# Two attentions and two feed-forward layers: q and k in two f32r parts on paired 64-row tiles, and attention loops unrolled

## The chip, the cores and the metric

The kernel runs on one core of a Trainium2 chip. The core has a matrix engine (PE), whose weight loads are shown as an engine of their own (PEld), a vector engine (DVE), a scalar engine (ACT), a general one (POOL) and a queue engine (SP) that issues transfers. The metric is the device time of one execution in microseconds, lower is better.

## The reference

All in float32, x is [2, 1024, 512]. Four layers, each on a layer norm of x and added to it:

```python
x = x + attn_a(ln(x))     # q = x Wq; latent = x Wc; k = latent Wk; v = latent Wv; rope on q, k;
                          # softmax(q k / 4) v, then Wo; 32 heads of 16, not causal
x = x + ffn(ln(x))        # x W + bias + a LoRA product
x = x + attn_b(ln(x))     # qkv = x w_attn + b; causal; scores / 16 + slope * (key - query)
x = x + ffn(ln(x))        # the same weights as before
```

## The kernel before

`project_a` makes q, k and v of attention a, `attention` runs attention a, `output_and_ffn` the output product, the feed-forward layer and the projection for b, then `attention` and `output_and_ffn` run again for b.

**Parts.** q and k are written to memory as three bf16 parts (high, middle, low) whose sum is the float32 value. A product q k is one matmul over 96 rows: six blocks of 16 rows, q's parts (0,0,0,1,1,2) against k's (0,1,2,0,1,0). In scores three more rows carry minus the maximum of the query (three bf16 parts against ones), in b three more the alibi ramp. ACT makes high and middle (`high`, `middle`), DVE the differences (`less_high`, `low`).

**Groups.** `attention` goes through 16 groups of four heads. The memory for a group's q, k and v is a slot, and there are three. A group has units: pairs of a half of the queries (512) and a block of 128 keys, 16 units in a and 12 in b, where masked blocks are left out. For each unit PE computes the scores of four heads (`scores`, L410, in two pairs of heads; each pair's exponential is one ACT instruction, L470, over two PSUM banks) and the value products (`values`, L427: plain f32, four heads on four 32-column tiles, two passes each).

**Maxima ahead.** The softmax needs each query's maximum before its scores. So 13 units (b) or 11 (a) ahead, PE computes q k with queries on the partitions (`maxima`, L369) in pieces of 128 queries by up to 512 keys, 64 pieces a group in a and 48 in b, and DVE reduces each to a column (L492). These pieces go through three PSUM banks (`MXB`): a piece waits for `piece_taken` of the one three before it. When half of a group is reduced, DVE takes the negated maxima, POOL splits them in parts (four instructions in a chain), PE turns them (L377, one item in the same three banks), DVE copies (L505) and one SP transfer writes them to the rows of the slot (L297).

**Order.** Each engine's order is written out by hand. In a unit PE does: scores of two heads, some pieces, scores of two heads, some pieces, values of the unit before, the other pieces. In a that is four pieces a unit. In b the diagonal blocks get a mask: a matmul of an identity and a 128x128 bf16 mask (L367, L408) ahead of the product in the same bank.

**Loops.** The first group is peeled, the next twelve are a hardware loop on each engine (on PE, DVE and SP four turns of three groups), the last three are straight code.

Of the kernel before, what the change touches and what calls it, by code (L numbers as in the profile page):

```python
# [37 lines left out]
Q_PARTS = (0, 0, 0, 1, 1, 2)  # L51
K_PARTS = (0, 1, 2, 0, 1, 0)
SROWS = DH * len(Q_PARTS)
SLOTS = 3
PEELED_FRONT = 1
LOOPED = 12


def wait_past(e, sem, value):

    if not isinstance(value, int) or value > 0:
        e.wait_ge(sem, value)


class Slot:
# [3 lines left out]
    QK_WORDS = GH * S // 2  # L69
    V_WORDS = 8 * GH * VW  # L70
    WORDS = 2 * QK_WORDS + V_WORDS

    def __init__(self, memory, rows, v_memory=None):

        self.rows = rows
        self.crow = rows - 3
        self.al = self.crow - SROWS
        n = self.QK_WORDS
        self.q = memory[0:rows, 0:n].bitcast(BF16)
        self.k = memory[0:rows, n:2 * n].bitcast(BF16)  # L80
        self.v = (memory[:, 2 * n:self.WORDS] if v_memory is None else v_memory).rearrange("p (k c) -> p k c", k=8)

    def load_q_row(self, e, r, q_d, g, loaded):

        e.dma_start(self.q[DH * r:DH * (r + 1), :].rearrange("d (n t) -> d n t", t=CHUNK),
                    q_d[Q_PARTS[r], bass.ds(g * 2 * GD, 2 * GD), :].rearrange("(n d) t -> d n t", d=DH),
                    ).then_inc(loaded, 16)

    def load_k_row(self, e, r, k_d, g, loaded):

        e.dma_start(self.k[DH * r:DH * (r + 1), :].rearrange("d (h t) -> d h t", h=GH),
                    k_d[K_PARTS[r], bass.ds(g * GD, GD), :].rearrange("(h d) t -> d h t", d=DH),
                    ).then_inc(loaded, 16)

    def load_q(self, e, q_d, g, loaded):
        for r in range(len(Q_PARTS)):
            self.load_q_row(e, r, q_d, g, loaded)

    def load_k(self, e, k_d, g, alibi_d, loaded):
        for r in range(len(K_PARTS)):  # L100
            self.load_k_row(e, r, k_d, g, loaded)
        if self.al:
            e.dma_start(self.k[SROWS:self.crow, :], alibi_d[bass.ds(g * self.al, self.al), :]).then_inc(loaded, 16)
# [5 lines left out]
    def set_rows(self, e, ones_d, done):  # L109

        e.dma_start(self.k[self.crow:self.rows, :], ones_d[0:3, :]).then_inc(done, 16)
        if self.al:
            e.dma_start(self.q[SROWS:self.crow, :], ones_d[0:self.al, :]).then_inc(done, 16)

# [1497 lines left out]
```

## Time and profile before

| | |
|---|---|
| runs | 1935.19, 1937.74, 1937.74 us, median 1937.74 |
| the profiled execution | span 1937.4 us, which is the time taken here as its own; 32402 instructions |
| PE | 1795.5 us busy (93%), weight loads 790.9 |
| DVE | 1408.8 (73%) |
| ACT | 982.5 (51%) |
| POOL | 147.3 (8%) |
| first projection | 0 to 184 us, the first maxima of attention a at 190.7 |
| attention a | first scores about 217 us, last output copy at 967 |
| middle stage | about 970 to 1247 us |
| attention b | 1251 to 1805 us |
| last stage | to 1937.4 |

Busy times are of instructions; records of matmuls overlap, so the distance from the start of one to the start of the next says more than their length. The granted clock is 1.00 at 2.4 GHz and 0.50 at 1.2 GHz.

### The profile page before, as it was taken

To read this page: it belongs to the slowest core of one execution; us is meant where nothing else is said; L and a number is where in the kernel's file an instruction comes from. 1 tells how busy PE (TensorE), PEld (TensorE's weight loads), DVE (VectorE), ACT (ScalarE), POOL (GpSimd) and SP (SyncE) were. 2 spreads that over 40 slices of the span, in tenths; PEclk is the share of its full clock that TensorE was granted. 3 is DMA by queue.
4 is the path that set the end of the run, shared out by engine and by line. 5 is a ranking of instruction groups with operands and counts; after the bars stand their busy time and mean duration, and the time that the engine had idled before them with its cause. 6 is when DMAs were issued, how large, how long until landed. Compare 5 with 4: busy or idle time off the path is not lost. (4 is left out here: it accounts for less than half of the span.)

```text
span 1937.4 us, 32402 instructions
## 1 busy us (share of the span) xinstructions
PE 1795.5 (93%) x10140; PEld 790.9 (41%) x10140; DVE 1408.8 (73%) x2559; ACT 982.5 (51%) x1233; POOL 147.3 (8%) x344
## 2 busy tenths in 40 slices
PE   5996999999999999999979999899989898998697
PEld 3543222222222222222235676634444443443376
DVE  2886988888888878888447454487868676775476
ACT  2543366666666666666711222236656465666310
POOL 2322100000000000000000000010000000002000
PEclk9888799999999999999989999879999999999798
DMA  6556613323323323330151335564436363441221
GB/s 193 160 140 185 87 38 57 56 46 58 56 45 58 61 38 64 51 50 10 53 165 39 109 109 139 140 99 73 81 57 97 52 90 64 76 77 42 85 97 65
DMA packets 143795, 158.10 MB, mean 82 GB/s; under 512 B 24135, under 2 KB 108359, under 8 KB 143559
## 3 DMA queue, kind: packets, MB, share of 16 engines
q1 hardware_dynamic: 141874, 150.68, 37.2%
q0 software_dynamic: 1760, 5.29, 1.6%
q8 instruction: 99, 1.62, 0.4%
q14 instruction: 62, 0.51, 0.1%
HBM read 99.55 MB, written 55.57 MB: 80 GB/s over the span
## 5 line engine op out<-in xcount | busy, mean ns | idle before, releaser
L492 DVE TENSOR_REDUCE a_mxp<-a_ps_m 128x1 f32<-128x512 f32 x1024 | 641.2, 683 | 98.2 <-PE a_ps_m L369 96.9
L470 ACT ACTIVATE a_p<-a_ps_s 128x1024 f32<-128x1024 f32 x512 | 495.5, 1021 | 245.7 <-PE a_ps_s L410 245.6
L492 DVE TENSOR_REDUCE b_mxp<-b_ps_m 128x1 f32<-128x512 f32 (+3 forms) x768 | 381.2, 551 | 131.1 <-PE b_ps_m L369 130.2
L470 ACT ACTIVATE b_p<-b_ps_s 128x1024 f32<-128x1024 f32 (+3 forms) x384 | 293.0, 808 | 236.5 <-PE b_ps_s L410 235.8
L369 PE MATMUL a_ps_m<-a_slot 96*128 96x512 bf16 x640 | 220.0, 387 | 0.0
L410 PE MATMUL a_ps_s<-a_slot 99*128 99x512 bf16 x640 | 193.9, 384 | 8.4 <-issue 8.3
L427 PE MATMUL a_ps_o<-a_p,a_slot 128*32 128x512 f32 x1280 | 170.5, 605 | 0.0
L369 PE MATMUL a_ps_m<-slot_memory 96*128 96x512 bf16 x384 | 141.9, 410 | 15.5 <-PEq L711 14.2
L367 PE MATMUL b_ps_m<-mask_qk,ident_bf 128*128 128x128 bf16 x512 | 118.3, 232 | 6.1 <-PEq L1170 5.0
L408 PE MATMUL b_ps_s<-mask_kq,ident_bf 128*128 128x128 bf16 x512 | 102.3, 225 | 22.9 <-DMA slot_memory<-b_cturned 12.6
L369 PEld LDWEIGHTS a_ps_m<-a_slot 96*128 96x128 bf16 x640 | 50.3, 97 | 178.4 <-DVE a_mxp L492 143.3
L410 PE MATMUL a_ps_s<-slot_memory 99*128 99x512 bf16 x384 | 114.7, 382 | 2.0 <-DMA slot_memory<-a_cturned 1.4
L427 PE MATMUL a_ps_o<-a_p,slot_memory 128*32 128x512 f32 x768 | 102.3, 605 | 0.7 <-ACT a_p L470 0.7
L621 PE MATMUL mid_ps<-mid_q_xnt,mid_w_qkv 128*128 128x512 f32 x384 | 90.9, 398 | 5.6 <-DVE mid_q_xnt L1434 5.6
L367 PEld LDWEIGHTS b_ps_m<-mask_qk,ident_bf 128*128 128x128 bf16 x512 | 50.9, 100 | 109.0 <-DVE b_mxp L492 91.7
L410 PEld LDWEIGHTS a_ps_s<-a_slot 99*128 99x128 bf16 x640 | 60.3, 99 | 85.4 <-issue 20.1
L369 PE MATMUL b_ps_m<-o_memory 99*128 99x512 bf16 (+3 forms) x288 | 91.3, 363 | 2.3 <-DVE b_mxp L492 2.2
L369 PEld LDWEIGHTS a_ps_m<-slot_memory 96*128 96x128 bf16 x384 | 31.2, 98 | 131.0 <-DVE a_mxp L492 97.3
L621 PEld LDWEIGHTS mid_ps<-mid_q_xnt,mid_w_qkv 128*128 128x128 f32 x384 | 73.4, 191 | 22.5 <-issue 7.2
L410 PE MATMUL b_ps_s<-o_memory 102*128 102x512 bf16 (+3 forms) x288 | 76.0, 332 | 1.1 <-ACT b_p L470 1.0
L369 PE MATMUL b_ps_m<-b_slot 99*128 99x512 bf16 (+1 forms) x240 | 71.4, 338 | 1.5 <-DVE b_mxp L492 1.5
L369 PE MATMUL b_ps_m<-slot_memory 99*128 99x512 bf16 (+1 forms) x240 | 70.5, 334 | 1.5 <-DVE b_mxp L492 1.5
(170 smaller groups left out, 2173.7 us busy)
## 6 DMA issues: line engine op xcount, KB each, us to landing
va_groups<-w_o SPq DMA_DIRECT2D x16, 512.0 KB, 3.7
vb_groups<-w_proj SPq DMA_DIRECT2D x16, 512.0 KB, 4.3
a_slot<-qa_parts SPq DMA_DIRECT2D x60, 128.0 KB, 4.6
ka_parts<-pa_parts SPq DMA_DIRECT2D x16, 384.0 KB, 2.6
qa_parts<-pa_parts SPq DMA_DIRECT2D x32, 192.0 KB, 3.2
a_slot<-ka_parts SPq DMA_DIRECT2D x48, 128.0 KB, 6.6
kb_parts<-slot_memory SPq DMA_DIRECT2D x16, 384.0 KB, 2.6
qb_parts<-slot_memory SPq DMA_DIRECT2D x32, 192.0 KB, 3.0
```

The lines of the kernel that those rows point to most:

```text
L367: pe.matmul(ps_m[:, bank, keys - P:keys], consts["ident_bf"][:, :], consts["mask_qk"][:, :], start=True, stop=False, skip_group_check=True)
L369: pe.matmul(ps_m[:, bank, 0:keys], q, k, start=not diagonal, stop=True, skip_group_check=diagonal).then_inc(piece_ready, 1)
L408: pe.matmul(ps_s[:, h, off:off + P], consts["ident_bf"][:, :], consts["mask_kq"][:, :], start=True, stop=False, skip_group_check=True)
L410: mm = pe.matmul(ps_s[:, h, off:CHUNK], k, q, start=not diagonal, stop=True, skip_group_check=diagonal)
L427: mm = pe.matmul(ps_o[VW * h:VW * (h + 1), off:CHUNK], slots[j].v[:, kt, VW * h:VW * (h + 1)], p_sb[:, (2 * u + h // 2) % NP, h % 2, off:C ...
L470: act.activation(p_sb[:, (2 * u + pair) % NP, :, off:CHUNK], ps_s[:, 2 * pair:2 * pair + 2, off:CHUNK], ACT.Exp, scale=scale).then_inc(exp ...
L492: dve.tensor_reduce(mxp[:, qt // 4, 4 * h + qt % 4, half:half + 1], ps_m[:, bank_of(g, j, i), 0:keys], AX.X, ALU.max).then_inc(piece_taken, 1)
L621: mm = pe.matmul(out, lhs[a](kc), rhs[b](kc), start=(n == 0), stop=(n == len(steps) - 1))
```

## The change

- q and k are stored in two f32r parts (high and the rest). A product is three blocks of 16 rows, q (0,0,1) against k (0,1,0): 48 rows, two rows for the maximum and in b two for the ramp. `middle` and one of the two subtractions go.
- The rows of the even heads lie at partitions 0 to 63, those of the odd heads at 64 to 127, so that a product uses a 64-row tile of PE and those of a pair of heads use both. Pieces are ordered in pairs (`e` is the head of the pair), the two of a pair write to different banks.
- A pair of pieces waits once, for the banks of both.
- A mask is two bf16 products over 64 rows, each for 64 columns.
- The pieces of a unit are split in two places instead of three, and counts are even: after the first scores and after the values.
- The turning product is plain f32 from 64 columns of parts; POOL's chain has two instructions; the shift is two transfers, one for each tile.
- The loops over groups are straight code on all engines, with constants in the waits.

```diff
-Q_PARTS = (0, 0, 0, 1, 1, 2)
-K_PARTS = (0, 1, 2, 0, 1, 0)
+Q_PARTS = (0, 0, 1)
+K_PARTS = (0, 1, 0)
 SROWS = DH * len(Q_PARTS)
+SHIFT_ROWS = 2
+ALIBI_ROWS = 2
+PAIR = 2
+ROW_TILE = P // PAIR
...
-    before_unit = [round(NPC * sum(columns[:u]) / sum(columns)) for u in range(NU + 1)]
+    before_unit = [2 * round(NPC * sum(columns[:u]) / sum(columns) / 2) for u in range(NU + 1)]
...
-                link(pool.tensor_tensor(cparts[:, 0, :], negm[:, :], zeros[:, :], ALU.subtract), 1)
-                link(pool.tensor_tensor(rest[:, :], negm[:, :], cparts[:, 0, :], ALU.subtract), 2)
-                link(pool.tensor_tensor(cparts[:, 1, :], rest[:, :], zeros[:, :], ALU.subtract), 3)
-                pool.tensor_tensor(cparts[:, 2, :], rest[:, :], cparts[:, 1, :],
+                pool.tensor_tensor(cparts[:, :, 0, :], split(negm[:, :]), split(zeros[:, :]),
+                                   ALU.subtract).then_inc(high_ready, 1)
+                pool.wait_ge(high_ready, g * 2 + (qh + 1))
+                pool.tensor_tensor(cparts[:, :, 1, :], split(negm[:, :]), cparts[:, :, 0, :].bitcast(F32),
                                    ALU.subtract).then_inc(parts_ready, 1)
...
+            def add_mask(to, mask, row):
+                tile = slice(row, row + ROW_TILE)
+                for half in range(2):
+                    pe.matmul(to[:, half * ROW_TILE:(half + 1) * ROW_TILE], mask[tile, half, :], half_ident[tile, :],
+                              start=(half == 0), stop=False, skip_group_check=True)
...
-                wait_past(pe, piece_taken, item(g, i) + (1 - MXB))
-                at = (qt // 4 * GH + h) * CHUNK + qt % 4 * P
-                q = slots[j].q[0:crow, at:at + P]
-                k = slots[j].k[0:crow, h * S + half * CHUNK:h * S + half * CHUNK + keys]
+                if e == 0:
+                    wait_past(pe, piece_taken, item(g, i + 1) + (1 - MXB))
+                row = ROW_TILE * e
+                q = slots[j].q[row:row + crow, qt // 4, pair, qt % 4 * P:(qt % 4 + 1) * P]
+                k = slots[j].k[row:row + crow, pair, half * CHUNK:half * CHUNK + keys]
...
-                for h in (2 * pair, 2 * pair + 1):
-                    k = slots[j].k[0:rows, h * S + kt * P:h * S + (kt + 1) * P]
-                    q = slots[j].q[0:rows, (qh * GH + h) * CHUNK + off:(qh * GH + h + 1) * CHUNK]
+                for e in range(PAIR):
+                    row = ROW_TILE * e
+                    k = slots[j].k[row:row + rows, pair, kt * P:(kt + 1) * P]
+                    q = slots[j].q[row:row + rows, qh, pair, off:CHUNK]
...
-                    first_cut = lo + (hi - lo + 2) // 4
-                    second_cut = first_cut + (hi - lo + 1) // 4
+                    cut = lo + PAIR * ((hi - lo + PAIR) // (2 * PAIR))
                     scores(s, j, u, 0)
-                    ahead(s, j, lo, first_cut, turn, n)
+                    ahead(s, j, lo, cut)
                     scores(s, j, u, 1)
-                    ahead(s, j, first_cut, second_cut, turn, n)
                     if u:
-                        values(s, j, u - 1, turn, n)
-                    ahead(s, j, second_cut, hi, turn, n)
-                values(s, j, NU - 1, turn, n)
+                        values(s, j, u - 1)
+                    ahead(s, j, cut, hi)
+                values(s, j, NU - 1)
...
-            with pe.Fori(0, LOOPED // SLOTS) as turn:
-                for n in range(PEELED_FRONT, PEELED_FRONT + SLOTS):
-                    step(turn * SLOTS + n, n % SLOTS, turn, n)
-            for s in range(PEELED_FRONT + LOOPED, NG):
-                step(s, s % SLOTS, None, s)
+            ahead(0, 0, 0, AHEAD)
+            for s in range(NG):
+                step(s, s % SLOTS)
```

## Rows read from the trace of the kernel before

**Rows 1.** Windows in the two attentions: busy time per engine, granted clock, DMA share, GB/s.
```profile
300.00:400.00 100.00, 100.00 (x558) 29.35 (x560) 88.07 (x150) 69.10 (x74) 4.35 (x20) 1.00 0.31 49
...
1300.00:1400.00 100.00, 98.71 (x817) 44.23 (x816) 78.54 (x167) 62.07 (x82) 5.22 (x24) 1.00 0.47 74
```
The first number is the length of the window, then come PE, PEld, DVE, ACT and POOL.

**Rows 2.** Timeline of PE in attention a, one unit: start, length, instructions merged.
```profile
399.59 1.06 PE L427 MATMUL a_ps_o<-a_p,slot_memory 128*32 128x512 f32 x8
...
401.03 0.60 PE L410 MATMUL a_ps_s<-slot_memory 99*128 99x512 bf16 x2
...
402.12 0.38 PE L369 MATMUL a_ps_m<-a_slot 96*128 96x512 bf16 x1
402.43 1.06 PE L427 MATMUL a_ps_o<-a_p,slot_memory 128*32 128x512 f32 x8
403.43 0.60 PE L369 MATMUL a_ps_m<-a_slot 96*128 96x512 bf16 x2
```

**Rows 3.** Timeline at the beginning of one value product.
```profile
402.43 0.16 PEld L427 LDWEIGHTS a_ps_o<-a_p,slot_memory 128*32 128x32 f32 x8 [0.43 <-issue]
402.43 0.64 PE L427 MATMUL a_ps_o<-a_p,slot_memory 128*32 128x512 f32 x4
```

**Rows 4.** Timeline at two hand-overs between PE and DVE.
```profile
201.58 1.87 DVE L492 TENSOR_REDUCE a_mxp<-a_ps_m 128x1 f32<-128x512 f32 x3
...
202.31 0.10 PEld L369 LDWEIGHTS a_ps_m<-slot_memory 96*128 96x128 bf16 x1 [0.49 <-DVE a_mxp L492]
```
```profile
394.58 0.60 PE L369 MATMUL a_ps_m<-a_slot 96*128 96x512 bf16 x2
...
395.01 0.69 DVE L492 TENSOR_REDUCE a_mxp<-a_ps_m 128x1 f32<-128x512 f32 x1 [0.35 <-PE a_ps_m L369]
```

**Rows 5.** Timeline of PE in the first projection: f32r products, steady and after a wait.
```profile
131.03 0.39 PE L621 MATMUL pa_ps<-pa_xnt,pa_wq_high 128*128 128x512 f32 x1
131.26 0.40 PE L621 MATMUL pa_ps<-pa_xnt_low,pa_wq_high 128*128 128x512 f32 x1
```
```profile
137.83 0.50 PE L621 MATMUL pa_ps<-pa_xnt,pa_wq_high 128*128 128x512 f32 x1
138.16 0.40 PE L621 MATMUL pa_ps<-pa_xnt_low,pa_wq_high 128*128 128x512 f32 x1
```

**Rows 6.** Weight loads by line: busy us, mean ns, and idle time before them.
```profile
L621 PEld LDWEIGHTS mid_ps<-mid_q_xnt,mid_w_qkv 128*128 128x128 f32 x384 | 73.4, 191 | 22.5 <-issue 7.2
...
L369 PEld LDWEIGHTS a_ps_m<-a_slot 96*128 96x128 bf16 x640 | 50.3, 97 | 178.4 <-DVE a_mxp L492 143.3 <-issue 2.1
```

**Rows 7.** Reductions of attention b by shape.
```profile
L492 DVE TENSOR_REDUCE b_mxp<-b_ps_m 128x1 f32<-128x512 f32 x384 | 253.7, 685 | 75.3 <-PE b_ps_m L369 75.3
...
L492 DVE TENSOR_REDUCE b_mxp<-b_ps_m 128x1 f32<-128x128 f32 x128 | 36.5, 285 | 34.9 <-PE b_ps_m L369 34.9
```

**Rows 8.** Timeline of PE in attention b: a mask and its product.
```profile
1405.08 0.22 PE L408 MATMUL b_ps_s<-mask_kq,ident_bf 128*128 128x128 bf16 x1
1405.14 0.22 PE L410 MATMUL b_ps_s<-o_memory 102*128 102x128 bf16 x1
```

**Rows 9.** Timeline of ACT at the second output copy of groups, attention a and b.
```profile
358.80 0.60 ACT L461 ACTIVATE out_a_sums<-a_ps_o 128x512 f32<-128x512 f32 x1 [1.49 <-PE a_ps_o L427]
...
405.10 0.60 ACT L461 ACTIVATE out_a_sums<-a_ps_o 128x512 f32<-128x512 f32 x1 [1.49 <-PE a_ps_o L427]
...
455.61 0.60 ACT L461 ACTIVATE out_a_sums<-a_ps_o 128x512 f32<-128x512 f32 x1 [1.49 <-PE a_ps_o L427]
```
```profile
1375.97 0.60 ACT L461 ACTIVATE out_b_sums<-b_ps_o 128x512 f32<-128x512 f32 x1 [1.07 <-PE b_ps_o L427]
...
1407.25 0.60 ACT L461 ACTIVATE out_b_sums<-b_ps_o 128x512 f32<-128x512 f32 x1 [1.08 <-PE b_ps_o L427]
...
1447.04 0.60 ACT L461 ACTIVATE out_b_sums<-b_ps_o 128x512 f32<-128x512 f32 x1 [1.08 <-PE b_ps_o L427]
```

**Rows 10.** Window before attention a's first scores.
```profile
200.00:210.00 10.00, 10.00 (x17) 1.69 (x17) 10.00 (x18) 0.00 (x0) 0.00 (x0) 0.50 1.07 148
```

**Rows 11.** The subtraction that goes, in the first projection.
```profile
L1031 DVE TENSOR_TENSOR pa_parts<-w_q,pa_parts 128x512 bf16<-128x512 f32 x32 | 25.1, 786 | 0.4
```

More of the change, by code:

```diff
@@ L146, in attention @@
     for qh in range(2):
-        for h in range(GH):
+        for pair in range(GH // PAIR):
             for qt in range(4 * qh, 4 * qh + 4):
@@ L151, in attention @@
                     if n > 0:
-                        pieces.append((h, qt, half, n))
+                        pieces += [(pair, e, qt, half, n) for e in range(PAIR)]
     NPC = len(pieces)
@@ L205, in sem @@
             return ctx.enter_context(nc.semaphore(f"{tag}_{name}"))
-        memories = memories + [sb(f"slot{n}", [P, Slot.WORDS], F32) for n in range(SLOTS - 1 - len(memories))]
-        slots = [first] + [Slot(memory, rows) for memory in memories]
+        slots = [first] + more + [
+            Slot(sb(f"slot_qk{n}", [P, Slot.QK_WORDS], F32R), sb(f"slot_v{n}", [P, Slot.V_WORDS], F32)[:, :], causal)
+            for n in range(SLOTS - 1 - len(more))]
         p_sb = sb("p", [P, NP, 2, CHUNK], F32)
@@ L332, in _, with loads, maxima @@
             shift_rows(0, 0, 0)
-            step(0, 0, loads=False)
-            with sp.Fori(0, LOOPED // SLOTS) as turn:
-                for n in range(SLOTS):
-                    step(turn * SLOTS + (n + PEELED_FRONT), (n + PEELED_FRONT) % SLOTS)
-            for s in range(PEELED_FRONT + LOOPED, NG):
-                step(s, s % SLOTS, ahead=s + 1 < NG, loads=s + SLOTS - 1 < NG)
+            for s in range(NG):
+                step(s, s % SLOTS, ahead=s + 1 < NG, loads=0 < s < NG - SLOTS + 1)
         @block.tensor
         def _(pe):
-            def loads(turn, n):
-                more = n // SLOTS + (1 if n % SLOTS else 0)
-                return more if turn is None else turn + more
-            def maxima(g, j, i, turn, n):
-                h, qt, half, keys = pieces[i]
-                bank = bank_of(g, j, i)
+            def loads(g):
+                return g // SLOTS + (1 if g % SLOTS else 0)
+            def add_mask(to, mask, row):
[3 more added lines that the diff above has]
+                              start=(half == 0), stop=False, skip_group_check=True)
+            def maxima(g, j, i):
+                pair, e, qt, half, keys = pieces[i]
                 if i == 0:
+                    if causal and g == 0:
+                        pe.wait_ge(masks_loaded, 16)
                     if j:
@@ L475, in step @@
                 copy_out(s, 1)
-            step(0)
-            with act.Fori(0, LOOPED) as turn:
-                step(turn + PEELED_FRONT)
-            for s in range(PEELED_FRONT + LOOPED, NG):
+            for s in range(NG):
                 step(s)
@@ L958, in _ @@
                     high(c, i)
-                    middle(c, i - 1)
                     if i == 1:
@@ L1341, in high @@
                                bias=bias_of(i)).then_inc(high_ready, 1)
-            def middle(c, i):
-                n = c * PT + i
-                banks.wait_drained(act, ("qk", c, i))
-                act.activation(parts[:, n % PARTS, 1, :], rest[:, n % MIX, :], ACT.Copy).then_inc(middle_ready, 1)
             if nxt:
@@ L1569, in shape_constants @@
             rot[i - DH // 2, i] = 1.0
-    key, query = np.arange(P)[:, None], np.arange(P)[None, :]
-    mask_kq = np.where(key > query, NEG, 0.0).astype(np.float32)
+    row, column = (np.arange(P) % ROW_TILE)[:, None], np.arange(P)[None, :]
+    masks = [np.where(row + half * ROW_TILE > column, NEG, 0.0) for half in range(2)]
+    masks += [np.where(column > row + half * ROW_TILE, NEG, 0.0) for half in range(2)]
+    masks = np.concatenate(masks + [np.where(row == np.arange(ROW_TILE)[None, :], 1.0, 0.0)], axis=1)
     base = 2 ** (-2 ** (-(np.log2(H) - 3)))
```

361 lines of the change are left out of this document (173 added, 188 removed).

## The prediction

> **What bounds the kernel now.** The table of windows gives the engine. In attention a PE is busy all of the time and DVE 88%, at full clock; in attention b PE 98.7%, DVE 79% [rows 1]. Both attentions together last from 190.7 to about 1806 us, so that is where the time is. The timeline of PE shows how: one unit (four f32 value products V, four maxima products M, four score products S) repeats every 2.84 us, 402.43 minus 399.59 [rows 2]. Of it V takes 1.00 (402.43 to 403.43), eight bf16 products 0.22 each (401.03 to 402.12 is five of them), and the step from the last M into V 0.31 where two M stand 0.22 apart, so entering V's 32-column tiles costs 0.09. 1.00 + 7 x 0.218 + 0.31 = 2.84. PE waits for nobody.
>
> Beside it DVE reduces four pieces a unit, and this pace matters once PE is quicker. The handshake is in two places [rows 4]. Before attention a's first scores only reductions run: one starts at 201.58 (three in 1.87 us, 0.68 long, 0.60 apart), and the weight load that waited for its bank begins at 202.31. So from the start of a reduction to the product that reuses its bank: **0.73 us**. The other way: product at 394.58 (the first of its two ends after 0.39), reduction at 395.01: **0.43 us**. DVE alone would need 4 x 0.60 = 2.40 us a unit.
>
> The page's last chain covers only the last stage and says nothing here. The third thing is the time from group to group, read at the second output copy [rows 9]: 46.3 us in a (358.80 to 405.10), 50.5 where the loop jumps back (405.10 to 455.61); 31.3 in b (1375.97 to 1407.25), 39.8 over the jump (1407.25 to 1447.04). Each attention has four turns of three groups, and the periods show three jumps inside plus the entries and exits, which are straight.
>
> **The change, part by part.**
>
> *Unrolling.* Straight-line groups at the ends of a and b run with the same 46.3 and 31.3 as looped ones, so straight code costs nothing I can see, and the jumps go: 3 x 4.2 + 3 x 8.5 = **-38 us**.
>
> *f32r products.* They stream as fast as bf16, nearly: 131.03 to 131.26 is 0.23 each [rows 5]. But the weight load takes 0.19 us instead of 0.10 [rows 6], and it shows where PE had waited: the product at 137.83 lasts 0.50 instead of 0.39, and the next starts 0.33 later, not 0.23. So a waited f32r product costs 0.10 more, to its reader and to what is behind it.
>
> *Pairs on two row tiles.* No row shows row tiles. The nearest are V's column tiles: eight weight loads in 0.16 us and the first four products together in 0.64 [rows 3], as long as one. The bounds for a pair are therefore 0.23 us (side by side) and 0.46 (one after the other); I take 0.23. The Trainium skill, TensorEngine Tiling (Array Packing), Key Properties, says that tiles load and multiply in parallel, and that changing the mode drains the array; the first would make the pair 0.23, the second is the 0.09 at V, which stays.
>
> *The handshake.* This is the part that decides. The first product of a pair waits for the banks of both. With three banks the second of them is free only when the first piece of the previous pair has been reduced. Before, DVE had two whole pieces in hand when PE was let go; now one. Between the starts of two M pairs there can be no less than: product 0.50, hand-over 0.04, then 0.73 from the reduction's start to the next product = **1.27 us**, whatever PE has to do meanwhile. PE is in order: behind the waiting M stand the next S and V, and behind them ACT.
>
> *Attention a.* A unit has two M pairs. From the first to the second PE passes M 0.33, S 0.23 + 0.09, V 1.00: 1.65 us, more than 1.27, so PE sets it. From the second over the next unit's S to the first: PE has 0.56 to do, so the handshake sets it: 1.27. Sum **2.92 us** a unit against 2.84. Sixteen units 46.7. Each of the two turning products in a group takes a bank between pairs; then both pieces of the previous pair must be gone, +0.60, and it is f32 and in another tile mode: 1.3 us a group against 0.9 now (46.3 - 45.4). So 48.0 against 46.3, times 15.5 groups = **+27 us**. Four reductions in 2.92 us leave DVE 82% busy: it is latency, not throughput. If the weight load were hidden the unit would be 2.72 (the 0.10 falls out of both intervals), if a pair were serial 3.4.
>
> *Attention b.* 24 M pairs a group. Mask products: today 0.06 us apart [rows 8]; now two bf16 of 64 columns ahead of each product, then an f32r load in the shadow of a short product. I estimate 0.17 us + the columns (0.05 to 0.21) for a diagonal pair when the two tiles interleave, up to twice that when they do not; today a diagonal pair is 0.23 to 0.55. The minimal interval of diagonal pairs, by the same sum with the reductions of 0.285 to 0.685 us [rows 7], is 0.78 at 128 keys, 0.96, 1.16, 1.34 at 512; 1.28 for the others. Walking the twelve units with the new counts of pairs (3,2,1,1,2,3,3,2,3,2,1,1): 13 intervals have nothing but at most a pair of scores between and take the minimum, 1.16 on average = 15.1 us; 11 have a score pair and V between, 1.68 on average = 18.5. Together **33.6 us** against 31.3, x 15.5 = **+36 us**. With interleaving absent +2.5 a group more (+40); with the load hidden -1.5 (-24).
>
> *Before the first scores* only M and reductions run, at half clock. Today this goes at DVE's pace, 0.60 a piece [rows 4, 10]. In pairs at 1.2 GHz: 0.61 of product, about 0.15 of waited load, 0.04, 0.73 = 1.5 us for two pieces, not 1.2: 22 pairs in a +6.5, 26 in b +5, and b now waits for the masks' transfer, +1.5: **+13 us**.
>
> *Parts.* In the first projection one of four DVE passes over each of 32 tiles goes, 25 us busy [rows 11], and one of ACT's. DVE sets the end only in the last chunk, where eight tiles x 0.60 = 5 us go, plus some of PE's 5 us of waits earlier; stores grow by a third. I take **-7** (0 to -15). In the middle stage PE is busy throughout, which covers the same saving: 0. The maxima's chain on POOL loses two of four links (0.6 us), all of it hidden; the shift takes two transfers of 0.8 us issue instead of one, needed 6.8 us after the turning product and ready about 5.9 after it: hidden, by a microsecond.
>
> Sum: -38 + 27 + 36 + 13 - 7 = **+31 us** on the profiled span of 1937.4, which is 0.3 below the median of the runs. Forecast **1968 us**, 1.6% slower.
>
> **Rivals.**
> 1. *The unrolling and cheaper products win* (0.23). If the waited load hides in the row tiles, the 0.10 falls away: a -23 instead of +27 (unit 2.72, 0.20 x 16 x 15.5 less), b +12, the beginnings +9: about 1890; half of that, 1929. For it: the loads of V's tiles overlap each other. Against: the 0.50 of a waited f32r product. Where handshake, beginnings and parts together lose less than the 38 us of the jumps, the change is faster.
> 2. *DVE's pace is all that is left* (0.04). If PE is never late, a unit is 4 x 0.60 = 2.40 us: 0.52 less than forecast, 8.3 a group, 129 in a, about 1830 in all. Against: with one piece in hand DVE must stand still while PE works through V. The Trainium skill, TensorEngine Tiling (Array Packing), PSUM Bottleneck, gives this rule: tiling speeds the products, not the emptying of PSUM.
> 3. *Pairs run one after the other, or bf16 masks between f32r products cost a drain* (0.12). Serial: a +0.46 a unit = +118, b +80: 2165. Only the masks: +40, 2010. For it: no row has row tiles, nor bf16 and f32r in turn.
> 4. *The clock stays at 1.2 GHz* (0.08). Before attention a's first scores PE counts as busy the whole time and is granted 0.50, which is 1.2 GHz [rows 10]; with scores in the mixture and no gaps it is 1.00, 2.4 GHz [rows 1]. The new units have a gap of 0.7 us in each, so it could rise later or fall. At 1.2 GHz a unit is about 4.6 us: +27 us a group; three groups late is +80, the whole of a +430. Against: V alone keeps the array at work for 1.0 us of each 2.9.
> 5. *The two sides cancel* (0.06): 1934 to 1941.
> Forecast 0.47, from 1942 to 2005.
>
> About 0.2% (4 us) is what a measurement here can tell from no change. Faster by more than that: 0.27; within: 0.06; slower: 0.47 + 0.12 + 0.08 = 0.67. Faster is rivals 1 and 2, 0.23 + 0.04. The range takes in rival 1 to its end and rivals 3 and 4 where they are mild: 1885 to 2060.
>
> **What would show it.** In windows of attention a: PE well under 100%, DVE about 82%; PE waiting for the reductions before every second M pair. Units 2.92 us apart; groups 48 and 33.6, all alike, no 50.5 or 39.8. Products of a pair a few ns apart (serial: 0.23). If units are 2.7, the waited load was wrong; if 3.4, the tiles; if the granted clock is under 0.95 between 260 and 960 us, rival 4. The mask products' spacing tells the estimate of 0.17.

## The result, and the profile after

The changed kernel takes 2051.59 us (median of four runs, 2042.08 to 2059.44) against 1937.74: ratio 1.0588, 95% interval 1.0553 to 1.0624. It is slower, as forecast, and inside the range, but the loss is 114 us, or 103 between the two profiled executions (spans 2040.3 and 1937.4), where 31 was forecast.

The table of windows, two stretches of attention a, two of attention b (window, PE, PEld, DVE, ACT, POOL, granted clock, DMA share, GB/s):

```profile
460.00:500.00 40.00, 36.31 (x160) 10.59 (x158) 24.97 (x41) 20.33 (x21) 0.44 (x2) 0.62 0.27 37
500.00:600.00 100.00, 81.23 (x536) 26.11 (x536) 86.24 (x141) 69.65 (x71) 1.75 (x8) 1.00 0.31 50
...
1310.00:1340.00 30.00, 15.98 (x100) 7.46 (x100) 20.64 (x43) 0.00 (x0) 4.02 (x10) 0.50 0.76 125
...
1470.00:1570.00 100.00, 82.68 (x960) 36.27 (x956) 72.62 (x154) 59.52 (x78) 2.64 (x12) 1.00 0.42 74
```

Where the clock is 1.00, PE is now busy 81 and 83% of the time, not 100 and 99 [rows 1]. And there are stretches like the first of these, in the middle of attention a, where it is not 1.00. Before there was no such stretch in the straight groups but one of 6.8 us in b's last two periods; else the clock fell only where the loop jumps back, for 3.4 us at each jump in a and 6.8 in b. From 260 to 960 us the mean granted clock is 0.93 (0.99 before), which is under the 0.95 that the prediction had named as the sign of rival 4.

The timeline of PE, one unit of attention a, which answers to [rows 2]:

```profile
509.30 0.50 PE L378 MATMUL a_ps_m<-slot_qk 48*128 48x512 f32 x2 [0.55 <-DVE a_mxp L493]
509.64 0.41 PE L418 MATMUL a_ps_s<-a_slot_qk 50*128 50x512 f32 x2
509.97 1.07 PE L435 MATMUL a_ps_o<-a_p,a_slot_v 128*32 128x512 f32 x8
510.97 0.50 PE L378 MATMUL a_ps_m<-slot_qk 48*128 48x512 f32 x2
511.31 0.40 PE L418 MATMUL a_ps_s<-a_slot_qk 50*128 50x512 f32 x2
512.25 0.50 PE L378 MATMUL a_ps_m<-slot_qk 48*128 48x512 f32 x2 [0.54 <-DVE a_mxp L493]
512.59 0.40 PE L418 MATMUL a_ps_s<-a_slot_qk 50*128 50x512 f32 x2
512.92 1.07 PE L435 MATMUL a_ps_o<-a_p,a_slot_v 128*32 128x512 f32 x8
```

A unit is 512.92 - 509.97 = 2.95 us (2.84 before). From the first pair of pieces over scores and values to the second: 510.97 - 509.30 = 1.67. From the second to the first of the next unit: 512.25 - 510.97 = 1.28, of which PE waits 0.54 for the reductions.

The timeline of ACT at the second output copy of groups, which answers to [rows 9]:

```profile
363.18 0.60 ACT L463 ACTIVATE out_a_sums<-a_ps_o 128x512 f32<-128x512 f32 x1 [1.42 <-PE a_ps_o L435]
...
414.14 0.60 ACT L463 ACTIVATE out_a_sums<-a_ps_o 128x512 f32<-128x512 f32 x1 [1.42 <-PE a_ps_o L435]
...
462.54 0.60 ACT L463 ACTIVATE out_a_sums<-a_ps_o 128x512 f32<-128x512 f32 x1 [1.42 <-PE a_ps_o L435]
...
521.97 0.60 ACT L463 ACTIVATE out_a_sums<-a_ps_o 128x512 f32<-128x512 f32 x1 [1.43 <-PE a_ps_o L435]
```
```profile
1425.60 0.60 ACT L463 ACTIVATE out_b_sums<-b_ps_o 128x512 f32<-128x512 f32 x1 [0.55 <-PE b_ps_o L435]
...
1467.08 0.60 ACT L463 ACTIVATE out_b_sums<-b_ps_o 128x512 f32<-128x512 f32 x1 [0.55 <-PE b_ps_o L435]
...
1501.12 0.60 ACT L463 ACTIVATE out_b_sums<-b_ps_o 128x512 f32<-128x512 f32 x1 [0.55 <-PE b_ps_o L435]
```

The periods are not alike. In a, 414.14 to 462.54 is 48.4 us, and eight of the fourteen periods between the first group's copy and the last group's are that; but 363.18 to 414.14 is 51.0 and 462.54 to 521.97 is 59.4. In b, 34.0 (1467.08 to 1501.12) and 41.5 (1425.60 to 1467.08). In each long one the granted clock is 0.50 for a while: 466 to 496.5 us in the group of 59.4. One unit there:

```profile
479.68 1.94 PE L435 MATMUL a_ps_o<-a_p,a_slot_v 128*32 128x512 f32 x8
481.54 0.79 PE L378 MATMUL a_ps_m<-a_slot_qk 48*128 48x512 f32 x2
482.14 0.63 PE L418 MATMUL a_ps_s<-a_slot_qk 50*128 50x512 f32 x2
483.21 0.79 PE L378 MATMUL a_ps_m<-slot_qk 48*128 48x512 f32 x2 [0.45 <-DVE a_mxp L493]
483.77 0.66 PE L418 MATMUL a_ps_s<-a_slot_qk 50*128 50x512 f32 x2
484.36 1.93 PE L435 MATMUL a_ps_o<-a_p,a_slot_v 128*32 128x512 f32 x8
```

4.68 us for the unit. The two traces side by side account for the 103 us:

| stretch | before | after | difference |
|---|---|---|---|
| start to a's first maxima | 190.7 | 175.6 | -15.1 |
| to a's first scores | 26.2 | 34.3 | +8.1 |
| to its first second copy | 49.3 | 56.5 | +7.2 |
| fifteen periods of a | 700.9 | 755.7 | +54.8 |
| middle stage to its last product | 280.3 | 282.1 | +1.8 |
| to b's first maxima (masks) | 5.4 | 7.1 | +1.7 |
| to b's first scores | 26.9 | 35.8 | +8.9 |
| to its first second copy | 33.8 | 44.6 | +10.8 |
| fifteen periods of b | 491.4 | 518.0 | +26.6 |
| last stage | 132.6 | 130.7 | -1.9 |

The two rows of periods hold the jumps that are gone. Against the periods of this kernel at full clock (48.4 and 34.0), the long ones alone add 36.0 us in a (six periods that sum to 326.4, less 6 x 48.4) and 15 in b (two of 41.5, less 2 x 34.0).

### The profile page after: what moved, and what is told of

It reads as the page before. It is cut to its first block and busy times, and to the rows that moved or that the text cites. A ratio compares the mean times of both kernels' runs of the same rounds, so it can differ in the third digit from the quotient of the medians.

```text
span 2040.3 us, 28808 instructions
## 1 busy us (share of the span) xinstructions
PE 1685.3 (83%) x11228; PEld 773.5 (38%) x11228; DVE 1395.5 (68%) x2495; ACT 986.5 (48%) x1169; POOL 119.7 (6%) x218
## 5 line engine op out<-in xcount | busy, mean ns | idle before, releaser
L378 PE MATMUL a_ps_m<-a_slot_qk 48*128 48x512 f32 x640 | 165.7, 514 | 86.5 <-DVE a_mxp L493 86.4
L435 PE MATMUL a_ps_o<-a_p,a_slot_v 128*32 128x512 f32 x1280 | 184.2, 649 | 0.0
L378 PE MATMUL a_ps_m<-slot_qk 48*128 48x512 f32 x384 | 110.8, 573 | 74.3 <-DVE a_mxp L493 62.3
L418 PE MATMUL a_ps_s<-a_slot_qk 50*128 50x512 f32 x640 | 137.0, 423 | 0.0
L354 PE MATMUL b_ps_m<-b_masks 64*128 64x64 bf16 x1024 | 63.9, 202 | 80.5 <-DVE b_mxp L493 72.5
L418 PE MATMUL a_ps_s<-slot_qk 50*128 50x512 f32 x384 | 84.6, 439 | 3.7 <-DMA slot_qk<-a_cturned 2.3
L378 PE MATMUL b_ps_m<-o_qk 50*128 50x512 f32 (+3 forms) x288 | 73.3, 501 | 12.5 <-DVE b_mxp L493 12.5
L418 PEld LDWEIGHTS a_ps_s<-a_slot_qk 50*128 50x128 f32 x640 | 65.1, 199 | 13.2 <-issue 12.7
L354 PE MATMUL b_ps_s<-b_masks 64*128 64x64 bf16 x1024 | 63.4, 201 | 3.3 <-ACT b_p L472 3.3
L435 PE MATMUL b_ps_o<-b_p,v_memory 128*32 128x512 f32 (+3 forms) x576 | 65.9, 535 | 0.1
```

Of the source, the lines that this page charges most:

```text
L354: pe.matmul(to[:, half * ROW_TILE:(half + 1) * ROW_TILE], mask[tile, half, :], half_ident[tile, :], start=(half == 0), stop=False, skip_gr ...
L378: pe.matmul(ps_m[:, bank_of(g, i), 0:keys], q, k, start=not diagonal, stop=True, skip_group_check=diagonal).then_inc(piece_ready, 1)
L418: mm = pe.matmul(ps_s[:, PAIR * pair + e, off:CHUNK], k, q, start=not diagonal, stop=True, skip_group_check=diagonal)
L435: mm = pe.matmul(ps_o[VW * h:VW * (h + 1), off:CHUNK], slots[j].v[:, kt, VW * h:VW * (h + 1)], p_sb[:, (2 * u + h // 2) % NP, h % 2, off:C ...
```

## The experiments

Twelve kernels; each ratio is to runs of the kernel before on the same chip (medians of 1935.35 to 1936.84 us). The changed kernel was not run again beside them, so a difference from it is taken across chips; where that matters, the traces are compared as well. The runs of three kernels differ among themselves by 2 to 4%, and for these their spread is given (pieces that wait for their own bank, more on one tile, bf16 over half the rows).

**Unrolling alone.** The kernel before, with straight code on all five engines.

```diff
-            with pe.Fori(0, LOOPED // SLOTS) as turn:
-                for n in range(PEELED_FRONT, PEELED_FRONT + SLOTS):
-                    step(turn * SLOTS + n, n % SLOTS, turn, n)
-            for s in range(PEELED_FRONT + LOOPED, NG):
+            for s in range(PEELED_FRONT, NG):
                 step(s, s % SLOTS, None, s)
```

> The kernel before (three bf16 parts, single pieces) with the loops over groups written out as straight code on all five engines and nothing else changed. Theory: the three jumps in each attention go, 3 x 4.2 in a and 3 x 8.5 in b, so 1900 us; groups of 46.3 and 31.3 us throughout, and a granted clock of 1.00 from 230 to 1240 us. Rival: straight code has a cost of its own (the periods of 51 and 59 us seen in the changed kernel come from it); then periods of 51 or more are seen here too and the time is 1920 or more.

Measured: 1897.26 us, ratio 0.9802 (0.9785 to 0.9820). A window of attention a:

```profile
500.00:600.00 100.00, 99.91 (x559) 29.22 (x561) 87.79 (x147) 68.81 (x74) 3.46 (x16) 1.00 0.29 49
```

Full periods of 46.3 (one 46.6) and 31.3; the clock is 1.00 from 218.5 to 955 us. Straight code costs nothing that shows, and the jumps were worth 39 us, the short falls of the clock at them included. So the rest of the change loses about 154 us.

**Single pieces.** The changed kernel, each piece with its own wait, in three places of a unit.

```diff
-    before_unit = [2 * round(NPC * sum(columns[:u]) / sum(columns) / 2) for u in range(NU + 1)]
+    before_unit = [round(NPC * sum(columns[:u]) / sum(columns)) for u in range(NU + 1)]
...
-                if e == 0:
-                    wait_past(pe, piece_taken, item(g, i + 1) + (1 - MXB))
+                wait_past(pe, piece_taken, item(g, i) + (1 - MXB))
...
-                    cut = lo + PAIR * ((hi - lo + PAIR) // (2 * PAIR))
+                    first_cut = lo + (hi - lo + 2) // 4
+                    second_cut = first_cut + (hi - lo + 1) // 4
                     scores(s, j, u, 0)
-                    ahead(s, j, lo, cut)
+                    ahead(s, j, lo, first_cut)
                     scores(s, j, u, 1)
+                    ahead(s, j, first_cut, second_cut)
                     if u:
                         values(s, j, u - 1)
-                    ahead(s, j, cut, hi)
+                    ahead(s, j, second_cut, hi)
```

> The changed kernel with the maxima pieces issued one by one as before: each waits for its own bank alone, and a unit's pieces stand at three places (after the first scores, after the second, after the values), odd counts allowed. Scores stay in pairs. Theory (the wait for two banks is what costs): DVE has pieces in hand again, PE's work in a unit is 1.09 + 0.46 + 4 x 0.23 = 2.47 us plus some waited loads of 0.10; a unit of 2.47 to 2.70, groups of 41 to 43.7 in a and about 31 in b, and fewer gaps in which the clock falls: 1860 to 1920 us. Rival (what the single pieces lose side by side costs more): four waited products of 0.33 and two pairs of 0.33 with 1.09 make 3.07, 51 us a group, over 2060.

Measured: 1943.07 us, ratio 1.0047 (1.0023 to 1.0071), so 108 us less than the change, but above the 1860 to 1920 expected. Second copies of two groups, and one unit on PE:

```profile
523.54 0.60 ACT L463 ACTIVATE out_a_sums<-a_ps_o 128x512 f32<-128x512 f32 x1 [1.50 <-PE a_ps_o L433]
...
568.31 0.60 ACT L463 ACTIVATE out_a_sums<-a_ps_o 128x512 f32<-128x512 f32 x1 [1.50 <-PE a_ps_o L433]
```
```profile
512.27 1.06 PE L433 MATMUL a_ps_o<-a_p,slot_memory 128*32 128x512 f32 x8
...
514.97 1.06 PE L433 MATMUL a_ps_o<-a_p,slot_memory 128*32 128x512 f32 x8
```

A unit takes 2.70, the upper end of what was expected, and a group of a 44.8 us, over the 43.7 expected but under the 46.3 of bf16. A group of b takes 32.2, still 0.9 over bf16's 31.3 (about 31 was expected). Of the drops of the clock in a only three short ones are left (periods of 45.9); in b there are three periods of 39.9 and two longer (41.5 and 47.3).

**Own bank, order unchanged.** The same wait without the three places.

```diff
-                if e == 0:
-                    wait_past(pe, piece_taken, item(g, i + 1) + (1 - MXB))
+                wait_past(pe, piece_taken, item(g, i) + (1 - MXB))
```

> The changed kernel with one edit: each piece waits for its own bank, order and places as they are. Theory: the first of a pair may start 0.60 earlier, the second still when the reduction before it ends; the shortest interval between pairs goes from 1.27 to DVE's 1.20 and the first product is no longer late: 0.07 to 0.25 us a unit, 1 to 4 us a group, 1980 to 2030 us. Rival (the order of the pieces is all that counts): groups of 48.4 and the same time within 0.5%.

Measured: 2217.07 us (2159.40 to 2234.16), which neither theory had. One unit at full clock and the same stretch as a window:

```profile
429.96 1.07 PE L433 MATMUL a_ps_o<-a_p,slot_memory 128*32 128x512 f32 x8
430.95 0.50 PE L376 MATMUL a_ps_m<-a_slot_qk 48*128 48x512 f32 x2
431.29 0.39 PE L416 MATMUL a_ps_s<-slot_qk 50*128 50x512 f32 x2
431.53 0.39 PE L376 MATMUL a_ps_m<-a_slot_qk 48*128 48x512 f32 x1
432.24 0.50 PE L376 MATMUL a_ps_m<-a_slot_qk 48*128 48x512 f32 x1 [0.32 <-DVE a_mxp L491]
432.24 0.73 PE L416 MATMUL a_ps_s<-slot_qk 50*128 50x512 f32 x2
432.90 1.07 PE L433 MATMUL a_ps_o<-a_p,slot_memory 128*32 128x512 f32 x8
```
```profile
400.00:480.00 80.00, 72.42 (x433) 25.97 (x429) 67.23 (x113) 56.70 (x59) 1.31 (x6) 1.00 0.35 54
...
500.00:560.00 60.00, 60.00 (x212) 20.02 (x204) 33.03 (x57) 26.57 (x27) 0.87 (x4) 0.50 0.23 38
```

The undisturbed unit is 2.94 us and the group 48.2, so the rival is right about the steady state: the place of the pieces counts, and the wait alone 0.2 us a group. But in a the clock first comes up only at 352 us, and then falls three times for 72 us each, with periods of 73. And here PE is busier than in the change (72.42 of 80 us is 91%, against 81). Its products are the same; what differs is that the two of a pair at 431.53 and 432.24 no longer run side by side. A clock that followed PE's busy time should have fallen less. That gave a second theory: it follows how much of the array works. This run alone doesn't show it, since the products of a unit and its length are nearly those of the change and yet the falls are longer.

**More scores.** The first pair of scores three times over, in attention a.

```diff
-                for e in range(PAIR):
+                for e in [x for _ in range(3 if pair == 0 and not causal else 1) for x in range(PAIR)]:
```

> The changed kernel in which PE computes the first pair of scores of each unit of attention a three times over into the same banks (work added, result unchanged); the two more take 0.46 us, in the place where PE otherwise waits 0.55 for the reductions. Attention b is as it was. Theory (the granted clock falls where PE has gaps): steady groups stay at 48.4 us, the periods of 51 to 59 go, granted clock 1.00 all through attention a, so about 36 us less: 2005 to 2015 although more is computed. Rival (the clock falls for another reason): the same drops in the same places, and the time the same or up to 30 us more where the products don't fit the gap.

Measured: 2000.72 us, ratio 1.0319 (1.0254 to 1.0384), 51 less than the change although more is computed. Between the two traces it is 31 (2040.3 and 2008.9), and all of it is in attention a, whose last copy is at 990.0 us and not 1022.0. All fourteen full periods of a are 48.8 or 48.9, and the clock is 1.00 from 216.5 to 950 us. So the long periods were the clock, and more products in the gap keep it up. The row of the added scores also gives the first price of a pair on two tiles:

```profile
509.63 0.87 PE L418 MATMUL a_ps_s<-slot_qk 50*128 50x512 f32 x6
```

Six products in 0.87 us, of which one alone is 0.39: so the last pair starts 0.48 after the first, 0.24 a pair.

**Pairs on one tile.** Both heads multiplied from the first tile's rows.

```diff
-                row = ROW_TILE * e
+                row = 0
                 q = slots[j].q[row:row + crow, qt // 4, pair, qt % 4 * P:(qt % 4 + 1) * P]
...
-                    row = ROW_TILE * e
+                    row = 0
                     k = slots[j].k[row:row + rows, pair, kt * P:(kt + 1) * P]
```

> The changed kernel with both heads of each pair multiplied from the rows of the first tile (partitions 0 to 63), so that the two products of a pair can't run side by side. The second head's result is that of the first (this part of the computation is changed); number, shape and waits of the instructions are the same. Theory (side by side is worth a whole product): where PE sets the interval, a pair of scores and a pair of maxima cost 0.23 more each, 2.13; where the handshake sets it, 1.27 stays; a unit of 3.40 us, groups of about 55.7 in a and 37 to 39 in b, and fuller PE so fewer clock drops: 2130 to 2200 us. Rival (pairs gain little): groups under 50 in a.

Measured: 3215.46 us, ratio 1.6598 (1.6568 to 1.6627). The window and the timeline of PE:

```profile
500.00:600.00 100.00, 100.00 (x289) 45.72 (x288) 45.84 (x74) 37.85 (x38) 0.87 (x4) 0.50 0.15 25
```
```profile
510.68 1.05 PE L378 MATMUL a_ps_m<-a_slot_qk 48*128 48x512 f32 x2
511.53 1.05 PE L418 MATMUL a_ps_s<-slot_qk 50*128 50x512 f32 x2
512.51 1.93 PE L435 MATMUL a_ps_o<-a_p,slot_memory 128*32 128x512 f32 x8
```

A pair takes 511.53 - 510.68 = 0.85 us at 1.2 GHz, two products of 0.43 one after the other. From a pair of scores to the values behind it is 512.51 - 511.53 = 0.98 us; in the change at the same clock it is 484.36 - 483.77 = 0.59. Side by side is worth 0.39 us there, close to a whole product, as the theory had it; at 2.4 GHz a serial pair was not seen. But the time is over 1000 us beyond the theory: in both attentions, for 1440 and 1110 us, PE is busy over 99% and the granted clock is 0.50 throughout.

**No masks.**

```diff
-                diagonal = causal and half == qt // 4
+                diagonal = False
...
-                diagonal = causal and P * kt >= CHUNK * qh
+                diagonal = False
```

> The changed kernel without the mask products of attention b, 32 pairs of heads a group (the masking is left out of the computation; nothing else is). Theory (masks are nearly free: the product starts 0.07 us after them): 0.07 to 0.24 us for each diagonal pair, 1 to 5 us a group in b, so 15 to 75 us less if the clock stays as it is; best guess 30, 2010 us. Attention a as in the changed kernel. Rival (the turn between bf16 and f32r costs a drain each time): over 5 us a group, groups under 29 in b.

Measured: 2082.61 us, ratio 1.0746 (1.0708 to 1.0784): less work and 31 us more than the change, where 30 less was the best guess. PE's timeline and two windows in b, and behind them the change's own pieces with masks:

```profile
1460.39 0.34 PE L378 MATMUL b_ps_m<-slot_qk 50*128 50x384 f32 x2
1461.38 0.50 PE L378 MATMUL b_ps_m<-slot_qk 50*128 50x512 f32 x2 [0.65 <-DVE b_mxp L493]
```
```profile
1443.00:1463.00 20.00, 14.92 (x116) 5.71 (x116) 15.36 (x32) 12.09 (x15) 0.44 (x2) 1.00 0.02 4
1463.00:1487.00 24.00, 21.45 (x100) 7.48 (x98) 12.83 (x27) 10.39 (x14) 0.44 (x2) 0.50 0.58 100
```
```profile
1501.37 0.23 PE L354 MATMUL b_ps_m<-b_masks 64*128 64x64 bf16 x4
1501.44 0.42 PE L378 MATMUL b_ps_m<-b_slot_qk 50*128 50x384 f32 x2
...
1502.52 0.24 PE L354 MATMUL b_ps_m<-b_masks 64*128 64x64 bf16 x4 [0.65 <-DVE b_mxp L493]
```

At full clock the theory holds: from the piece of 384 keys to that of 512 it is 0.99 us, against 1.15 with masks (1501.37 to 1502.52). But with the mask products gone PE is busy 75% at full clock (83% with them), and the clock falls in every full group of b: periods of 38.2 and 40.3 in turn. What the masks cost is less than what they keep up. Attention a is that of the change, on another chip, and the falls are there too: five periods of 50.9 to 59.4 among the fourteen. The next kernel ran beside it on the same chip, with the threefold scores in a, and has none (48.8 or 48.9 in all).

**Filled beginnings.** With the threefold scores, a plain f32 product after each pair before the first scores.

```diff
                 pe.matmul(ps_m[:, bank_of(g, i), 0:keys], q, k, start=not diagonal, stop=True,
                           skip_group_check=diagonal).then_inc(piece_ready, 1)
+                if fill and e == 1:
+                    pe.matmul(ps_o[:, 0:P], consts["ident"][:, :], consts["ident"][:, :], start=True, stop=True)
...
-            ahead(0, 0, 0, AHEAD)
+            ahead(0, 0, 0, AHEAD, True)
```

> As the run with the first scores of attention a computed three times, and besides, while only maxima run before each attention's first scores, one plain f32 product of 128 columns into the still empty values bank after each pair (26 in b, 22 in a; work added, result unchanged). Theory (the cold clock at the beginnings comes from gaps and small products): granted clock up during the maxima, at the latest with the first scores: b's first scores to its second output copy 15 to 25 us shorter, 1970 to 1985 us. Rival: the clock is still 0.50 until the values run and the products only add to PE: same as without them or up to 10 us more.

Measured: 2023.49 us, ratio 1.0435 (1.0408 to 1.0462). The theory fell. The clock stays 0.50 during the maxima, and in b it comes up at 1415 us, 98 after the first scores; without the fill, in the trace of the threefold scores, it came up 8 us after them (30 in that of the change). b's first scores to its second copy are 52.3 us, not 44.6 or 36.8. The time is above the 1970 to 1985 expected and above the 2000.72 without the fill. Why the clock came up so late here is open.

**Single pieces and fill.** Single pieces, the same fill, and in b the first scores of a unit without a mask twice.

```diff
-                for e in range(PAIR):
+                for e in [x for _ in range(2 if pair == 0 and causal and not diagonal else 1) for x in range(PAIR)]:
```

> The kernel with single pieces, with the same fill before each attention's first scores, and in attention b the first scores of the four units a group without a mask computed twice (work added, result unchanged). Theory (what is left in b with single pieces, 44 us in periods above 32.2, is clock): all b groups 32.2 to 33.0, granted clock 1.00 through both attentions, beginnings 10 to 20 us shorter: 1875 to 1895, under the unrolled bf16 kernel. Rival: the added work costs 14 us in b and the drops stay, 1950.

Measured: 1908.58 us, ratio 0.9864 (0.9846 to 0.9883): 34 less than single pieces alone, and 14 above the range expected for it. All of the first thirteen periods of b are 32.2, none longer, so the twofold scores cost nothing that shows and take the clock's losses away. The beginning of b was not shorter as a whole: from its first maxima to its second copy it is 78.9 us, against 74.5 with single pieces alone; the maxima take 9.9 longer, and the stretch behind the first scores 5.5 less (40.5 us; 34.1 in the unrolled bf16 kernel).

**Each attention its own.** Attention a and its projection from the single pieces, all else from the unrolled bf16 kernel.

```diff
-            project_a(nc, env, first)
+            project_a_f32r(nc, env, first)
...
-            attention(nc, "a", False, DH ** -0.5, consts, env["qa_d"], env["ka_d"], env["va_d"],
-                      env["oa_d"], env["za_d"], None, ins["ones"], [], first, output,
+            attention_a(nc, "a", False, DH ** -0.5, consts, env["qa_d"], env["ka_d"], env["va_d"],
+                      env["oa_d"], env["za_d"], None, env["ones_a"], first, [], output,
```

> A new combination with nothing left out: attention a and its projection as in the kernel with single pieces (two f32r parts, 64-row tiles), the middle stage, attention b and the last stage as in the unrolled bf16 kernel. Theory (the parts add up): attention a ends at 922 us as there, and from there to the end 942 us as in the unrolled bf16 kernel: 1866 us, 1860 to 1875; faster than all kernels so far. Rival: the clock falls more often in attention a in this build, 1880 to 1900.

Measured: 1863.70 us, ratio 0.9625 (0.9606 to 0.9643), the fastest of all. Attention a's last copy is at 923.3 us, as expected; its groups take 44.7 or 44.8 (two 45.9), those of b 31.3 (one 31.5).

**A wait for two banks in bf16.** The unrolled bf16 kernel with one edit.

```diff
-                wait_past(pe, piece_taken, item(g, i) + (1 - MXB))
+                if i % 2 == 0:
+                    wait_past(pe, piece_taken, item(g, i + 1) + (1 - MXB))
```

> The unrolled bf16 kernel in which every second piece waits for its own bank and the next one's, and the piece after it for nothing; order and places as before. Theory (a wait for two banks takes DVE's piece in hand, whatever the type): PE is no longer 100% busy; groups over 47 us in a and over 32 in b; 1915 to 1980 us. Rival (with a bf16 product and pieces spread over three places the wait is hidden): 46.3 and 31.3 as without it, 1897 us.

Measured: 2049.22 us, ratio 1.0587 (1.0563 to 1.0611), more than the theory's top. Second copies of two groups and a window:

```profile
533.03 0.60 ACT L454 ACTIVATE out_a_sums<-a_ps_o 128x512 f32<-128x512 f32 x1 [1.74 <-PE a_ps_o L423]
...
584.69 0.60 ACT L454 ACTIVATE out_a_sums<-a_ps_o 128x512 f32<-128x512 f32 x1 [1.74 <-PE a_ps_o L423]
```
```profile
500.00:600.00 100.00, 94.08 (x500) 24.13 (x499) 79.69 (x132) 63.09 (x67) 2.59 (x12) 1.00 0.31 49
```

51.7 us a group in a and 35.5 in b, at full clock in all of them. One wait, moved by one piece, costs 152 us here, with nothing else changed: the piece that DVE had in hand is gone, and PE is no longer busy 100%. It needs neither f32r nor row tiles nor the two places.

**More on one tile.** The added scores all on the first tile.

```diff
-                for e in range(PAIR):
+                for e in ((0, 0, 0, 1) if pair == 0 and not causal else (0, 1)):
```

> The changed kernel in which the first head's product of the first pair of scores of each unit of attention a is computed three times (the second head's once): two products more on the first tile alone, one after the other, the same 0.46 us of PE as in the run with three pairs, with half the array under them. Theory (the clock follows how much of the array works, not how long PE is busy): some periods over 50 us stay in a; 2005 to 2045. Rival (busy time counts): all groups 48.8 to 49 as with three pairs, 1990 to 2014.

Measured: 2007.01, 2020.40, 2030.82 and 2052.54 us; the ratio, 1.0407 (1.0364 to 1.0449), is that of the first three. That is between the change and the three pairs, but the runs of the three pairs (1989.60 to 2014.30) overlap with these, so it is the traces that part them. A window here, and the same of the kernel with three pairs:

```profile
500.00:600.00 100.00, 95.99 (x592) 37.84 (x596) 84.42 (x138) 65.19 (x70) 1.74 (x8) 0.98 0.30 51
```
```profile
500.00:600.00 100.00, 95.89 (x664) 38.00 (x666) 85.36 (x140) 65.29 (x70) 1.75 (x8) 1.00 0.30 49
```

PE is busy 96% in both. With half of the array under the added products, the clock drops for 3.4 us in every second group (periods of 48.8 and 50.1 in turn, one of 51.6); with all of it, never in the steady groups, in either of the two traces that have the three pairs (this one and that of the filled beginnings).

**bf16 over half the rows.**

```diff
-                q = slots[j].q[0:crow, at:at + P]
-                k = slots[j].k[0:crow, h * S + half * CHUNK:h * S + half * CHUNK + keys]
+                q = slots[j].q[0:crow // 2, at:at + P]
+                k = slots[j].k[0:crow // 2, h * S + half * CHUNK:h * S + half * CHUNK + keys]
```

> The unrolled bf16 kernel with the products q k over the first half of their rows only (48 of 96 for the maxima and 48 of 99 for the scores; in b 49; this leaves half of each product and the shift by the maximum out of the computation, and the exponential's scale is 256 times smaller to keep it in range). Number, columns and order of the instructions are the same. Theory (the clock follows how much of the array works): PE busy about 100% and still a granted clock of 0.50 over long stretches; groups of 60 us and more in a, over 2100 us. Rival (PE's busy time decides): clock 1.00, groups of 46.3 and 31.3, about 1897 us.

Measured: 2740.30 us (2676.80 to 2759.14). Two windows of attention a and two second copies:

```profile
500.00:600.00 100.00, 99.89 (x563) 28.45 (x561) 88.11 (x148) 69.12 (x74) 3.46 (x16) 1.00 0.37 59
900.00:1000.00 100.00, 100.00 (x299) 22.33 (x301) 50.30 (x80) 39.96 (x40) 2.59 (x12) 0.50 0.16 24
```
```profile
971.95 0.60 ACT L453 ACTIVATE out_a_sums<-a_ps_o 128x512 f32<-128x512 f32 x1 [4.12 <-PE a_ps_o L422]
...
1058.82 0.60 ACT L453 ACTIVATE out_a_sums<-a_ps_o 128x512 f32<-128x512 f32 x1 [4.12 <-PE a_ps_o L422]
```

At full clock the group is 46.1 us, so the products take as long as over 96 rows, and PE is busy 99.9%. Yet for some 575 us of a and for nearly all of b the clock is 0.50, and the group up to 86.9. So the rival is out: PE's busy time alone does not decide. But the second theory is not the whole of it either: from 471.7 to 891.6 us the clock is 1.00 under the same work. And the numbers in the products differ as well, which this run can't tell from their rows.

## Why the prediction was wrong in its size, point by point

- **Unrolling, -38.** Right: 39 by the run with nothing else.
- **The handshake.** Right, in its mechanism and its numbers: interval of 1.28 for 1.27, the other 1.67 for 1.65, unit 2.95 for 2.92, group 48.4 for 48.0, b 34.0 for 33.6, DVE 86% for 82. Against the unrolled bf16 kernel the fifteen periods are 67.2 us longer in a (755.7, 688.5) and 53.1 in b (518.0, 464.9). Without the 36.0 and the 15 of the long ones that is +31 and +38, where +27 and +36 stood. The bf16 kernel with the wait for two banks shows that the wait is enough, and the two runs with own waits show where the cure is: the wait alone gives 0.2 us a group of a, with the pieces spread over three places it is 3.6.
- **Pairs side by side.** Right: 0.24 us a pair for 0.23, and 0.85 at 1.2 GHz when serial. Rival 3 is out, masks and all: the product starts 0.07 after its masks (1501.37 to 1501.44 in the change), and they cost about 0.16 (1.15 less 0.99) where the handshake sets the pace.
- **Parts, -7.** Too small: the first maxima start 15.1 us earlier, of which the parts are 12.0, by the unrolled bf16 kernel (187.6 to 175.6). That is near the end of the range given, 15.
- **Beginnings, +13.** Too small. What they name was nearly right: maxima before the first scores +8.1 in a for 6.5 and +8.9 in b for 5, masks' transfer +1.7 for 1.5, together 18.7. What they leave out is what comes behind: from first scores to the first second copy +7.2 and +10.8, where the clock stays at 0.50 longer than before (17 us after the first scores for 3 in a, 30 for 6 in b); in b this stretch is 44.6 us, and 36.8 in each of the runs with three pairs and with more on one tile, whose attention b is the same but where the clock came up 8 us after the first scores.
- **The clock, the step that failed.** The sum has no term for it: it took 1.00 for all steady groups, with the reason "V alone keeps the array at work for 1.0 us of each 2.9", and gave rival 4 a chance of 0.08 and its price only as whole groups in the cold. In the trace it comes as short falls, from 7 to 31 us: 36.0 us in a and 15 in b, and a good part of the 18 us behind the first scores. The price of a cold unit, 4.6 us, was right (4.68). Forecast +31 plus those 51 is +82; the beginnings' 24 more (8.1 + 7.2 + 1.7 + 8.9 + 10.8 less 13) and the steady groups' 6 more (31 + 38 less 63) make +112; the parts take back 8, and the jumps 1. That leaves the +103 measured between the two traces.

Rivals 1, 2 and 5 are out, and rival 4 is what came on top of the forecast, in a milder form than it was priced in. With the pieces placed one by one a unit falls to 2.70, near the 2.72 that rival 1 had for a hidden load; but there the load still shows (the waited products last 0.50), and what changed is the wait.

Why the clock falls: the three pairs of scores show that more products cure it. One tile at 100% busy, bf16 over 48 rows at 100% busy, and 96% busy with half or all of the array under the added products show that PE's busy time alone doesn't decide. That it is how much of the array is at work fits these runs, but is argued and not shown to be the whole: the kernel with pieces that wait for their own bank has the same products in a unit of 2.94 us and loses the clock for 72 us at a time where the change loses 7 to 31, and bf16 over 48 rows held 1.00 for 420 us. The change takes from both, busy time and array: its products use 96 rows as before, but a pair does in 0.24 us what took 0.44, and the time won is spent waiting for DVE. The Trainium skill, TensorE: Matmul & The Clock Gate, Part 1: The HAM clock gate, says that the clock follows how busy the engine has been. The window of 100 us at PE 100.00 and clock 0.50 disagrees, if busy is read as the profile's busy time; the measurement decides. The same page of the Trainium skill has a section, A second HAM failure mode: psum-queue depth-cycling; a clock that swings because the engine idles for moments between groups of products while it cycles through PSUM banks is what it tells of, and what the change shows (waits of 0.54 to 0.55 us before every second pair). It does not cover the two kernels that are busy 100% at 0.50. Whether the number of rows or of columns, or the data, weighs more was not tried.

Open: why the clock came up 98 us after b's first scores with the filled beginnings and 8 us after them without the fill. In the traces of four kernels with the same code in b it is 30, 8, 8 and, with the fill, 98 us, so no cause for it should be read off a single one.

## What to carry to other kernels

A wait for two buffers at once, in a ring of three, takes away the piece that the other engine had in hand: it added 5.4 us to groups of 46.3 with nothing else changed. So give each its own wait and put the requests apart. Before packing products side by side, ask who consumes them: if that is the bound, the time won is idle time, and an emptier array can lose its clock as well. And test parts of a change alone: the unrolling (-39), the two f32r parts with single pieces in attention a (another -34) were gains that the whole hid.

## What the runs showed of the hardware

- PE can be busy 100% for over 1000 us at a granted clock of 0.50, with products over 48 to 52 rows beside value products over 128 (both heads on one tile; bf16 over half the rows). In the second of these it was also 1.00 for 420 us. Over 96 to 102 rows, with the same instructions, it was 1.00 in every steady group of the unrolled kernel.
- Less work can take longer: without the masks' products 31 us more. More work can take less: with two more pairs of scores a unit in one attention 51 us less (31 between the traces).
- An f32r product over 48 to 50 rows on one of two tiles takes as long as one over 128 rows (0.39 us), and a pair on two tiles goes every 0.24 us, as one did (0.23); its waited weight load shows 0.10 to 0.11, as on the whole array.
